# Ranking 20,000 edges within 100 buckets: one column of edges at a time, with the counts of the buckets on partitions

## The reference, cut to what matters

```python
xn = layernorm(x)                                    # x: 1250 x 1024
x = x + gnn0(xn, edge_index) + linear_attention0(xn)     # edge_index: 20,000 edges (src, dst), sorted by dst
x = x + moe_top2_of_8(layernorm(x))
xn = layernorm(x)
W = zeros(1024, 1024).at[src, dst].add(edge_weight)      # the same 20,000 edges
x = x + xn @ W.T + gnn_bias + linear_attention1(xn)
x = x + gated_mlp(xn(x))
```

## Time and profile before

| | |
|---|---|
| median of 3 runs | 2587.33 us (2587.26 to 2588.2) |
| the profiled execution's own time | 2587.87 us |
| span of the profiled execution, first to last instruction | 2585.8 us |
| instructions | 33801 |
| busy PE / PEld / DVE / ACT / POOL | 2240.4 / 1990.0 / 1627.6 / 1018.3 / 254.4 us |
| mean granted TensorE clock | 0.939 of 2.4 GHz |
| `graph_sort`, start of the span to the first DMA of `embed` | 0 to 105.85 us |

### The profile page before, as it was taken

The page is one execution under the profiler, slowest core; times in us unless marked ns, Lnnn a source line. Parts: engine busy times, 40 slices in busy tenths (PEclk is TensorE's granted clock), DMA queues, the critical chain, the costliest instruction groups (busy, mean ns, idle before and its releaser), DMA issues. The chain is left out here.

```text
span 2585.8 us, 33801 instructions
## 1 busy us (share of the span) xinstructions
PE 2240.4 (87%) x12654; PEld 1990.0 (77%) x12654; DVE 1627.6 (63%) x2675; ACT 1018.3 (39%) x1617; POOL 254.4 (10%) x259
## 2 busy tenths in 40 slices
PE   1689999996995999944499999995989999989898
PEld 1679999995884777744388888884779999978697
DVE  8865656656876788843499999986743333335422
ACT  1512322223763454411488888872111222221120
POOL 0257770000000000002000000002100000000000
PEclk9899999998997999955799999997999999999899
DMA  1241211123341000066545554415411111134314
GB/s 48 70 160 38 67 39 40 45 72 106 119 144 56 9 9 9 21 222 222 186 175 204 178 205 152 163 41 212 157 57 37 60 51 37 50 115 141 101 54 134
DMA packets 104211, 259.04 MB, mean 100 GB/s; under 512 B 17103, under 2 KB 44102, under 8 KB 104046
## 3 DMA queue, kind: packets, MB, share of 16 engines
q1 hardware_dynamic: 93230, 235.88, 26.6%
q0 software_dynamic: 10816, 20.99, 2.9%
HBM read 291.69 MB, written 84.49 MB: 145 GB/s over the span
## 5 line engine op out<-in xcount | busy, mean ns | idle before, releaser
L2131 DVE TENSOR_TENSOR ex_wl<-ex_raw,ex_wh 128x1024 fp32r<-128x1024 f32 x324 | 375.6, 1218 | 59.0 <-ACT ex_wh L2198 58.4
L2198 ACT ACTIVATE ex_wh<-ex_raw 128x1024 fp32r<-128x1024 f32 x324 | 329.3, 1058 | 94.2 <-DMA ex_raw<-in_experts 59.5
L1423 DVE TENSOR_TENSOR m_kvf<-m_bank,m_bkv 128x256 f32<-128x256 f32 (+1 forms) x160 | 67.9, 424 | 222.3 <-PE m_bank L1328 222.2
L1089 POOL DMA_INDIRECT scratch_slots<-pay,idx x160 | 198.9, 1243 | 57.6 <-issue 57.6
L1328 PE MATMUL m_bank<-m_w_lo,xh 128*128 128x256 f32 (+1 forms) x1280 | 178.3, 282 | 0.0
L1328 PE MATMUL m_bank<-m_w_hi,xl 128*128 128x256 f32 (+1 forms) x1280 | 177.0, 281 | 0.0
L1328 PE MATMUL m_bank<-m_w_hi,xh 128*128 128x256 f32 (+1 forms) x1280 | 177.0, 281 | 0.0
L1589 PE MATMUL gl_bank<-gl_gh,gl_al 125*125 125x512 f32 x400 | 158.7, 397 | 8.7 <-DVE gl_al L1757 8.7
L1328 PEld LDWEIGHTS m_bank<-m_w_lo,xh 128*128 128x128 f32 (+1 forms) x1280 | 163.9, 186 | 0.1
L1328 PEld LDWEIGHTS m_bank<-m_w_hi,xl 128*128 128x128 f32 (+1 forms) x1280 | 162.3, 186 | 0.0
L1328 PEld LDWEIGHTS m_bank<-m_w_hi,xh 128*128 128x128 f32 (+1 forms) x1280 | 161.4, 186 | 0.0
(11 more groups left out here) (409 smaller groups left out, 5226.6 us busy)
## 6 DMA issues: line engine op xcount, KB each, us to landing
ex_raw<-in_experts SPq DMA_DIRECT2D x324, 512.0 KB
raw<-in_qkv SPq DMA_DIRECT2D x48, 512.0 KB, 5.7
xr<-scratch_res SPq DMA_DIRECT2D x45, 512.0 KB, 4.1
scratch_res<-xr SPq DMA_DIRECT2D x36, 512.0 KB, 4.4
ex_xr<-scratch_seats SPq DMA_DIRECT2D x27, 512.0 KB, 3.7
scratch_served<-ex_y SPq DMA_DIRECT2D x27, 512.0 KB, 2.6
scratch_at<-xr SPq DMA_DIRECT2D x48, 209.0 KB, 2.5
o_ar<-scratch_at SPq DMA_DIRECT2D x18, 512.0 KB, 5.0
```

Source lines behind the costliest of these rows:

```text
L1089: e.indirect_dma_start(dram["slot_rows"], bass.IndirectOffsetOnAxis(idx[:, k:k + 1].bitcast(U32), 0), pay[:, k, :], None).then_inc(scat.se ...
L1423: e.tensor_tensor(f, bank[KVB + s % 3][0:r, 0:W2], bkv[0:r], ALU.add)
L2131: return e.tensor_tensor(wl[:, n % RING], raw[:, unit[1]], wh[:, n % RING].bitcast(F32), ALU.subtract)
L2198: e.activation(wh[:, n % RING], raw[:, unit[1]], ACT.Copy).then_inc(high.sem)
```

## The change

All of it is in `graph_sort` (and one new HBM scratch, `keys`, of 4 x 5,000 bf16, in `build`). The prefix sum and the loop over buckets go. The edges' order is now by columns: rank = edges of the bucket in earlier columns + edges of the bucket higher up in the same column.

- `hot` is laid out 125 x (160 columns x 100 buckets) and made in four quarters of 40 columns. For this ACT writes `keyb` four times beside itself (`key4`), as the compare reads runs of four.
- Within a column: PE multiplies a strict triangle by 5 columns of `hot` at a time (500 moving columns, bf16, 32 products), ACT copies each result to bf16 (`loc`, two quarters deep), and DVE multiplies it by `hot`, adds the two halves of the buckets and reduces over the last 50, which leaves `rank`.
- Before the column: 160 products `hot[:, k]` (as weights, 100 columns) by one column of ones leave the counts in PSUM, buckets on partitions, columns along the free axis. DVE makes a prefix sum over 160 elements and splits it in high and low part; with the spill base of the bucket, found by one triangle product, it is `gm`, 100 buckets x 160 columns x 4.
- To bring `gm` back to the edges, the one-hot is needed with buckets on partitions. SP writes `keyb` to HBM in four DMAs, reads each quarter back to 100 partitions (10,000 B each), and DVE compares it in place with the partition number (`turn`, `hot_t`). PE gathers with 160 products, `hot_t` of column k (125 weight columns, 40 elements apart) by 4 columns of `gm`.
- The table `off` is made from a product as well, while the gather runs; the chain that makes `idx` comes after the gather, with two more operations.
- On SP's queue the eight weight loads of `embed` and the fill of the slots are now issued behind these eight DMAs. POOL's constants are in bf16, and the unit matrix is gone.

```diff
+    SHIFT, QC, G = 17, EK // 4, 5
+    QN = QC // G
+        QS = range(EK // QC)
+        groups = [(q, g) for q in QS for g in range(QN)]
+        hot = sb("hot", [EP, EK, NBUCK], BF16)
+        loc = sb("loc", [EP, 2, QC, NBUCK], BF16)
+        hot_t = sb("hot_t", [NBUCK, len(QS), EP * QC], BF16)
+        gm = sb("gm", [NBUCK, EK, 4], BF16)
...
         @block.sync
+            e.wait_ge(*keyed["key"])
+            for q in QS:
+                e.dma_start(dram["keys"][q], keyb[:, cols(q)]).then_inc(keys_out.sem, 16)
+            for q in QS:
+                e.wait_ge(*keys_out[QS[-1]])
+                e.dma_start(hot_t[:, q], dram["key_row"][q:q + 1].broadcast_to([NBUCK, EP * QC])).then_inc(keys_in[q].sem, 16)
             for s in range(KC):
                 ahead.load(e, then, s)
...
         @block.tensor
-            (the two products of the counts, the loop over 100 buckets)
+            for n, (q, g) in enumerate(groups):
+                if g == 0:
+                    e.wait_ge(*hot_done[q])
+                if n >= 3:
+                    e.wait_ge(*local[groups[n - 3]])
+                k0 = q * QC + g * G
+                e.matmul(pl[n % 3][0:EP, 0:G * NBUCK], tri[0:EP, 0:EP], flat(hot[:, k0:k0 + G]),
+                         start=True, stop=True).then_inc(ranked.sem)
+                for k in range(k0, k0 + G):
+                    m = e.matmul(pt[0:NBUCK, k:k + 1], hot[:, k], ones[0:EP, 0:1], start=True, stop=True)
+            m.then_inc(counted.sem)
+            e.wait_ge(*beyond["nch"])
+            e.matmul(pn[0:NBUCK, 0:1], tri[0:NBUCK, 0:NBUCK], nch[:], start=True, stop=True)
+            e.matmul(pn[:, 1:2], ones[0:NBUCK], nch[:], start=True, stop=True).then_inc(spread.sem)
+            e.wait_ge(*based["based"])
+            for q in QS:
+                e.wait_ge(*turned[q])
+                t = hot_t[:, q].rearrange("b (p k) -> b p k", k=QC)
+                for k in range(QC):
+                    m = e.matmul(got[:, q * QC + k], t[:, :, k], gm[:, q * QC + k], start=True, stop=True)
+                if q == 0:
+                    (two products for the table off)
+            m.then_inc(gathered.sem)
...
         @block.scalar
-            (the loop over 100 buckets)
+            e.activation(key4[:], keyb[:].unsqueeze(2).broadcast_to([EP, EK, 4]), ACT.Copy).then_inc(fours.sem)
+            for n, (q, g) in enumerate(groups):
+                e.wait_ge(*ranked[q, g])
+                if q >= 2 and g == 0:
+                    e.wait_ge(*summed[q - 2])
+                e.activation(flat(loc[:, q % 2, g * G:(g + 1) * G]), pl[n % 3][0:EP, 0:G * NBUCK],
+                             ACT.Copy).then_inc(local.sem)
...
         @block.vector
-            (one compare of 16,000, the prefix sum of 16,000, the loop over 100 buckets)
+            for q in QS:
+                val = key4[:, cols(q)].unsqueeze(2).broadcast_to([EP, QC, NBUCK // 4, 4])
+                e.tensor_tensor(by4(hot[:, cols(q)]), row, val, ALU.is_equal).then_inc(hot_done.sem)
+
+            def turn(q):
+                e.wait_ge(*keys_in[q][q])
+                e.tensor_scalar(hot_t[:, q], hot_t[:, q], bid[0:NBUCK, 0:1], None, ALU.is_equal).then_inc(turned.sem)
+
+            for q in QS:
+                o = loc[:, q % 2]
+                half = NBUCK // 2
+                e.wait_ge(*local[q, QN - 1])
+                e.tensor_tensor(o, o, hot[:, cols(q)], ALU.mult)
+                d()
+                e.tensor_tensor(o[:, :, 0:half], o[:, :, 0:half], o[:, :, half:NBUCK], ALU.add)
+                d()
+                e.tensor_reduce(rank[:, cols(q)], o[:, :, 0:half], AX.X, ALU.add).then_inc(summed.sem)
+                if q + 1 < len(QS):
+                    turn(q)
+
+            e.wait_ge(*counted["counted"])
+            (copy of the counts, prefix sum over 160, 9 small operations: bsi, bhi, blo, nch, gm[0:2])
+            turn(QS[-1])
+            e.wait_ge(*spread["spread"])
+            (excl, spill, past, gm[2:4] -> based; ends -> shown; the table off)
+            e.wait_ge(*gathered["gathered"])
+            e.scalar_tensor_tensor(pos[:], got[:, :, 0], float(P), rank[:], ALU.mult, ALU.add)
...
+            e.tensor_tensor(rank[:], got[:, :, 1], pos[:], ALU.add)
...
+            e.scalar_tensor_tensor(idx[:], idf[:], float(NCH), hif[:], ALU.mult, ALU.add)
```

More of the change, by code:

```diff
@@ L867, in graph_sort @@
 def graph_sort(nc, dram, idx, pay, spill, raw, then):
-    SHIFT = 17
+    SHIFT, QC, G = 17, EK // 4, 5
     OVER = -(-2 ** SHIFT // TP)
-    assert all(v * OVER >> SHIFT == v // TP for v in range(N))
+    QN = QC // G
+    assert all(v * OVER >> SHIFT == v // TP for v in range(N)) and EP <= P and EK < 256 and EP < 256
     with Phase(nc, "gs") as p:
         sb, ctx = p.sb, p.ctx
+        QS = range(EK // QC)
+        groups = [(q, g) for q in QS for g in range(QN)]
         ld = p.raises("ld", ["src", "dst", "wgt"], 16)
         ahead = Ahead(p, raw, range(KC))
[L878 to L882, removed]
+        fill, offs, keys_out = p.raises("fill", ["fill"], 16), p.raises("offs", ["off"], 16), p.raises("keys_out", QS, 16)
+        keys_in = [p.raises(f"keys_in{q}", [q], 16) for q in QS]
+        consts = p.raises("consts", ["ones", "rows", "tri"])
+        keyed, fours, hot_done, ranked, local = (p.raises(n, o) for n, o in (
+            ("keyed", ["key"]), ("fours", ["key"]), ("hot_done", QS), ("ranked", groups), ("local", groups)))
+        counted, shown, spread, based, gathered = (p.raises(n, [n]) for n in (
+            "counted", "shown", "spread", "based", "gathered"))
+        summed = p.raises("summed", QS)
+        turned, beyond, found, offset = (p.raises(n, o) for n, o in (
+            ("turned", QS), ("beyond", ["nch"]), ("found", ["bk"]), ("offset", ["offset"])))
         src, dst, wgt = sb("src", [EP, EK], I32), sb("dst", [EP, EK], I32), sb("wgt", [EP, EK])
@@ L909, in graph_sort @@
         off = sb("off", [P, 2, 2], I32)
[L910 to L912 removed]
+        pl = [ctx.enter_context(nc.psum_tensor(f"gs_pl{i}", [P, 512], F32)) for i in range(3)]
+        pt = ctx.enter_context(nc.psum_tensor("gs_pt", [P, EK], F32))
+        pn = ctx.enter_context(nc.psum_tensor("gs_pn", [P, 4], F32))
+        pg = ctx.enter_context(nc.psum_tensor("gs_pg", [P, 1024], F32))
+        got = pg[0:EP, 0:4 * EK].rearrange("p (k f) -> p k f", f=4)
+        cols = lambda q: slice(q * QC, (q + 1) * QC)
         block = p.block()
@@ new lines, in _ @@
+            m.then_inc(counted.sem)
[9 more added lines that the diff above has]
+                if q == 0:
+                    e.wait_ge(*shown["shown"])
+                    for t in range(2):
+                        n = e.matmul(pn[:, 2 + t:3 + t], ends[:, t * P:(t + 1) * P], ones[0:NBUCK, 0:1],
+                                     start=True, stop=True)
+                    n.then_inc(found.sem)
@@ L996, in _ @@
[L996 to L1001, removed]
+            e.wait_ge(*consts["rows"])
+            e.wait_ge(*fours["key"])
+            by4 = lambda t: t.rearrange("p k (b f) -> p k b f", f=4)
@@ L1002, in _ @@
+            e.wait_ge(*counted["counted"])
+            e.tensor_copy(cnt[:], pt[0:NBUCK])
+            d()
+            e.tensor_tensor_scan(incl[:], cnt[:], cnt[:], 0.0, ALU.add, ALU.max)
+            d()
+            e.tensor_scalar(tot[:], incl[:, EK - 1:EK], float(HOME * P), 0.0, ALU.subtract, ALU.max)
+            e.tensor_tensor(bsi[:], incl[:], cnt[:], ALU.subtract)
             d()
             e.tensor_scalar(toti[:], tot[:], float(P - 1), None, ALU.add)
+            e.tensor_scalar(bhi[:], bsi[:], 7, None, ALU.arith_shift_right)
@@ L1016, in _ @@
[L1016 to L1051, removed]
@@ L1052, in _ @@
-            e.tensor_copy(rank[:], hi7[:])
-            d()
-            e.scalar_tensor_tensor(idx[:], idf[:], float(NCH), rank[:], ALU.mult, ALU.add)
+            e.tensor_copy(nch[:], toti[:]).then_inc(beyond.sem)
+            e.tensor_copy(gm[:, :, 0], bhi[:])
+            e.tensor_copy(gm[:, :, 1], blo[:])
+            turn(QS[-1])
+            e.wait_ge(*spread["spread"])
+            e.tensor_copy(excl[:], pn[0:NBUCK, 0:1])
+            e.tensor_copy(spill[:], pn[:, 1:2])
+            d()
@@ L1057, in _ @@
+            e.tensor_tensor(past[:], excl[:], nch[:], ALU.add)
+            e.tensor_copy(gm[:, :, 2:4], excl[:].unsqueeze(2).broadcast_to([NBUCK, EK, 2])).then_inc(based.sem)
+            d()
+            e.tensor_scalar(ends[:], cid[0:NBUCK], past[:, 0:1], None, ALU.is_ge).then_inc(shown.sem)
+            e.wait_ge(*found["bk"])
+            e.tensor_copy(bk[:], pn[:, 2:4])
+            d()
             e.tensor_scalar(bkb[:], bk[:], 103.0, None, ALU.mult)
```

85 lines of the change are left out of this document (39 added, 46 removed).

## The result

| | before | changed |
|---|---|---|
| median (range, runs) | 2587.26 us (2584.46 to 2588.2, 5) | 2573.8 us (2570.01 to 2574.34, 5) |
| ratio of the medians | | 0.9945, 95% interval 0.9931 to 0.996 |
| the profiled execution: its time, its span | 2587.87, 2585.8 us | 2570.46, 2568.3 us |
| `graph_sort`, start of the span to the first DMA of `embed` | 0 to 105.85 us | 0 to 92.14 us |

The change makes the kernel 13.5 us faster. The forecast was 2555, 32 us faster: the sign was right, the size was not, and 2573.8 lies outside the range of 2545 to 2572.

The account below looks back on a forecast made before the run. `graph_sort` was taken to have the core to itself and end at a barrier. Its new steps summed to an end at 73.7 us instead of 105.85, 32.1 us less, giving 2555 us; range 2545 to 2572.

Parts of the forecast that it names:

- the clock of the prediction: Running time through the new `graph_sort`, started at 9.1 us and added step by step to its end at 73.7 us.
- Dear weight loads: Gather: weight columns 80 bytes apart load at the fp32 pass's 0.21 us, gather 34 us, kernel 2571; chance 0.15.
- The reading of the clock for a gather of small products: Gather: PE busy with products of few columns stays at 1.2 GHz, so 0.11 us a product, 17.6 us.
- The rival of the high clock: Gather at 0.057 us a product, 9.1 us for 17.6, first PE quarter 2 us shorter: 2545 to 2547; chance 0.17.
- PE's quarters: Within-column products and counts: 7.0 us a quarter at the low clock, just hidden beside DVE's 7.35.
- the prediction's sign: Gather: the profile after would show a granted clock of 0.5 in that stretch.
- Moving `raw`: Weight loads and fill queued behind the key reads on SP: costs nothing, as they have until 70 us and more.
- Nothing else moves: Outside `graph_sort`: `embed` starts with weights loaded as before, the scatter writes the same rows; only 32.1 us come off.
- The slower case: Gather: each strided weight column takes four clock times, 0.42 us a product, 67 us, kernel 2604; chance 0.03.

Follow-up runs that it names:

- e2_steps: Changed kernel plus eight groups of 24 unused products behind the gather, varying the step between weight columns and the moving columns; 2602.26 us, single execution.
- e4_kmajor: Changed kernel with PE turning each quarter of the keys before HBM, so the gather's weight columns lie side by side; 2551.24 us, ratio 0.9859.
- e5: e4_kmajor plus 54 unused products of 500 columns between the last count and the gather; 2552.93 us.
- e3: Changed kernel plus 54 unused products of 500 columns between the last count and the gather; 2572.8 us, ratio 0.9943.

## Why the prediction was off

The direction and the path were right: the phase ends at a barrier and each microsecond of it is one of the program (13.7 us less in the phase, 13.5 in the medians). The forecast was 32.1. Point by point, with the clock of the prediction:

| step | predicted | measured |
|---|---|---|
| first compare starts | 9.1 us | 8.28 |
| four compares | 8.5 us | 8.68 |
| DVE starts the first multiply | 18.5 | 18.03 |
| multiply, add, reduce, turn | 2.24, 1.20, 2.25, 1.5 | 2.24, 1.20, 2.23, 1.51 |
| a group on PE (500 columns, five counts) | 0.87 | 0.87 |
| DVE waits for `keys` | none | none |
| gather starts | 51.4 | 50.40 |
| gather, 160 products | 0.11 each, 17.6 | 0.23 each, 36.8 |
| `idx` chain; its end to `embed` | 3.7; 0.7 | 3.9; 1.0 |
| first DMA of `embed` | 73.7 | 92.14 |

- **The step that failed** is "The weights are 125 columns, so a product is 0.057 us at the high clock and 0.11 at the low one by the same rows". The rows that it leaned on the earlier trace rows have their weight columns side by side, and the change lays them 80 bytes apart. The count of columns was taken as the whole price of a load. e2_steps shows that the distance doubles it between 8 and 16 bytes, and e4_kmajor, which changes the layout and adds only the turning of the keys, gets the 17.3 us and 2551 for which the prediction had 17.6 and 2555. This one term is 36.8 - 17.6 = 19.2 us too small. The phase missed by 18.4; the rest are small terms of both signs, 0.8 us of them the early start.
- The mechanism was on record as a rival, "Dear weight loads", with 34 us for the gather and 2571 for the kernel: 36.8 and 2573.8 came. It got 0.15 for want of a row. Its price was borrowed from fp32 passes with contiguous weights (0.21 us a pass). That it is low by only a tenth is luck, as those rows say nothing of distance; and with the 2.8 us between the two the result lies just past the range's end of 2572. Where no row shows an operand of the new form, 0.48 for the price of the old form was too much.
- The reading of the clock for a gather of small products was right. The rival of the high clock falls twice: no profile shows such a gather at 2.4 GHz from start to end, and even one started there (e5) fell back in about 4 us. In the changed kernel it would hardly have helped: forty products with far columns, about half of them at 1.00, took 0.224 us each, against 0.229 (e3).
- PE's quarters: right, 8 groups of 0.867 are 6.9 us beside DVE's 7.17, but the granted clock of the windows doesn't show it. In the changed kernel it reads 1.00 from 12 to 50 us, though 500 columns take 0.45 us, 1.1 columns a nanosecond, which is the level of 1.2 GHz. It reads 1.00 in the gather too, where the prediction's sign was 0.5, and that sign can't be read there. In these profiles the column shows a low clock only after a first change has been recorded; the spacing of products with a known number of columns is the safer reading. In the kernel before, the 1.00 from 61 to 97 us is real. Its loop over the buckets starts with a turn every 0.74 us, and from 60.5 us on, where the trace records its first change, a turn takes 0.38:

```profile
59.19 0.81 PE L952 MATMUL gs_prank<-gs_pick,gs_eye 125*125 125x160 f32 x2
...
60.99 0.47 PE L952 MATMUL gs_prank<-gs_pick,gs_eye 125*125 125x160 f32 x2
```

So the change took PE from a loop at the high clock, with products of 160 columns, to a gather at the low one.

- The start at 8.28 in place of 9.1, which I had as unchanged, comes for the most part from the loads of the edges: DVE's first operation, which waits for them, starts at 4.92 us in place of 5.52. That `raw` no longer goes out beside them is the likely cause; no run puts it back, so it isn't shown. It is 0.8 us gained by a step that I costed at nothing.
- Moving `raw` was free, as said: its issues stood for 19 us behind the reads of `keys`, and were over at 31 us.
- "Nothing else moves" was not quite so. The profiled spans differ by 17.5 us, the phase by 13.7. Of the rest 1.6 is the second fall of the clock in `embed` that only the profile of before has; the remaining 2 us lie spread over the later phases, within the range of single runs (4 us). The medians, 13.5 apart, are the number to go by.
- The slower case (0.31 us a product or more) did not come: from 16 to 78 bytes apart the price stays at 0.21 to 0.23 us.

## What to carry to other kernels

Price a product on PE by its weight load as well as its moving columns, and the load by where its columns lie: before a transposed or strided slice is given to PE as weights, see whether the layout can be turned where it costs little, as four products of 40 x 125 at the start of the phase did here for 19.5 us of gather. When a term rests on a row whose operands have another layout than the new ones, treat the term as open, and let the range hold both prices fully. After a change that leaves one engine waiting for a chain of small products, look for work in front of the chain that it doesn't need: moving DVE's last quarter behind it was worth another 6 us.

## What the runs showed of the hardware

- A load of 125 bf16 weight columns with a small product behind it, on 100 rows, clock at the level of 1.2 GHz: 0.107 us a product with columns 2 or 4 bytes apart, 0.116 at 8, 0.229 at 16, 0.212 at 64, 0.227 at 78. What in the chip makes the step between 8 and 16 bytes no run shows, and distances between the two, or fp32 weights, weren't tried. The Trainium skill ("TensorE: Matmul & The Clock Gate", section "LDWEIGHTS (loading the stationary operand)") gives the load a time in proportion to its number of columns alone. The same 125 columns cost the same at 2 and 4 bytes, as it says, 0.009 us more at 8, and about double from 16 bytes on, where the trace doesn't agree.
- The near load goes with the granted clock (0.057 and 0.107 us), the far one hardly (0.224 over forty products that began at 1.00, 0.229 at 0.50).
- In e3 and in e5 the granted clock fell from 1.00 to 0.50 some 4 us into the gather, behind the last product of 500 columns, with PE busy without a break before and after.
- Products of 500 columns alternating with five of one column, PE busy from 12 to 38 us without a break, stayed at the level of 1.2 GHz; in e3 and e5, with 44 products of 500 columns behind them, PE reached 2.4 GHz. The loop of the kernel before (160 columns) reached it at 60.5 us.
- Two-byte `tensor_scalar` of 5,000 elements took 1.51 us, 0.3 ns an element, against 0.56 for the two-source operation (2.24 us for 4,000). The prediction had chosen this value against one of 2.76; no row of before had shown it.
